# Turning gathered rows before the edge product is added, and making that product already turned, in a four-layer graph network on one core

## The chip, the core and the metric

One Trainium2 chip, one NeuronCore of it. The metric is the device time of one execution of the whole program in microseconds; lower is better. The engines are TensorE (PE, with its weight loads as PEld), VectorE (DVE), ScalarE (ACT), GpSimd (POOL) and SyncE (SP, which here only issues DMAs).

## What is computed

Four graph layers over 6250 nodes of 96 features and 206,250 edges sorted by destination, each layer followed by a layer norm of `x + layer(x)`. The change touches the edge stages of the second and third layer:

```python
# layer 1 (sum of messages)
msg  = relu(x[src] + edge_attr @ We + be)          # edge_attr: 206250 x 32, We: 32 x 96
aggr = segment_sum(msg, dst)
h    = x + aggr ...
# layer 2 (maximum of messages), twice: W1_*, then W2_*
msg  = x[src] @ W_msg + edge_attr @ W_edge
agg  = segment_max(msg, dst)                        # -inf -> 0
out  = leaky_relu(agg + x @ W_root + b)
```

Layers 0 and 3 are attention layers with edge stages of their own, which the change leaves alone.

## The kernel before

The kernel is written out fully (no loops on the chip), with waits on semaphores placed by hand; each engine runs its own list in program order.

There are five long edge stages. The first (line 789 gathers its rows) and the last (line 1843) belong to the attention layers. The three between them are made by one function, `edge_pass`: pass `e` for the sum with a ReLU (its tiles are named `e_...` in the profile, as are those of the two attention stages), passes `e2a` and `e2b` for the two maxima. Between the stages lie short node stages.

`edge_pass` walks over the edges in `NS` = 202 steps of 1024 edges. In a step:

- GpSimd issues 8 indirect DMAs (line 1151), each of which gathers 128 rows of 96 floats of `x_tab` by a column of `src_cols` into `got`. There are `RS` = 3 buffers of `got`; step s waits until the add of step s-3 has read its buffer.
- TensorE multiplies edge attributes by the edge weights (line 1168): two matmuls, the attributes as weights of the array and a block-diagonal `edge_w` (four copies of the 32 x 96 weights) streamed, 384 columns each, into the PSUM tile `EA`, edges on the partitions.
- VectorE does four things in order: `add` (line 1187: `EA` in PSUM plus `got` in SBUF, into `emsg`), `forward` (line 1193: 32 x 32 blocks turned, `emsg` into the PSUM tile `F`, so that edges lie along the free dimension), `scan` (line 1202: three scans of 256 columns, the bf16 mask in SBUF, the messages read from `F` in PSUM, into `run`), and `back` (line 1210: `run` turned back into `out`).
- In pass `e` ScalarE applies the ReLU to `emsg` between `add` and `forward` (line 1227).
- SyncE loads the attributes (one DMA a step) and the mask (four DMAs every second step) and stores `out`.

Every fourth step TensorE also makes the product of one tile of 128 nodes (line 1164, or a transposition of `X` in pass `e`) into a free corner of `EA`, and VectorE takes it out just ahead of the `add` (lines 1181 to 1185). 49 node tiles are done so in a pass.

## Time and profile before

| | |
|---|---|
| time, median of 3 runs | 11235.1 us (11234.0 to 11235.58) |
| span of the profiled execution | 13179.5 us |
| time of the profiled execution outside its span | not recorded apart |
| POOL busy | 8151.7 us (62%), 8551 instructions |
| DVE busy | 6535.8 us (50%), 10237 instructions |
| PE, PEld busy | 4527.1 us (34%), 3022.1 us (23%) |
| ACT busy | 1994.5 us (15%) |
| granted TensorE clock, mean | 0.541 of full speed |

The profiled execution is 1944 us longer than the median of the timed runs. Durations of single instructions are those of this one execution; where engines wait in it, the timed runs need not wait as long. The profile names, for each group of instructions, the busy time, the mean duration of one, and the idle time of the engine just before it with what ended that idle time: "issue" is time in which the engine waited for nothing that the profile shows, "remote" is a semaphore whose giver it did not find.

### The profile page before, as it was taken

To read this page: it belongs to the slowest core of one execution; us is meant where nothing else is said; L and a number is where in the kernel's file an instruction comes from. 1 tells how busy PE (TensorE), PEld (TensorE's weight loads), DVE (VectorE), ACT (ScalarE), POOL (GpSimd) and SP (SyncE) were. 2 spreads that over 40 slices of the span, in tenths; PEclk is the share of its full clock that TensorE was granted. 3 is DMA by queue.
4 is the path that set the end of the run, shared out by engine and by line. 5 is a ranking of instruction groups with operands and counts; after the bars stand their busy time and mean duration, and the time that the engine had idled before them with its cause. 6 is when DMAs were issued, how large, how long until landed. Compare 5 with 4: busy or idle time off the path is not lost. (4 is left out here: it accounts for less than half of the span.)

```text
span 13179.5 us, 81573 instructions
## 1 busy us (share of the span) xinstructions
PE 4527.1 (34%) x15877; PEld 3022.1 (23%) x15877; DVE 6535.8 (50%) x10237; ACT 1994.5 (15%) x4360; POOL 8151.7 (62%) x8551
## 2 busy tenths in 40 slices
PE   3354455555222222232222222222222234434443
PEld 3244344444110111111111111111111123333332
DVE  9543344444544454454445455444544544444445
ACT  3233333333100000010000000000000022222223
POOL 1455555555676666656666666766666666666665
PEclk7555555555555555555555555555555555555555
DMA  2355555555333333323333332333333222222222
GB/s 76 106 155 154 149 152 155 153 159 152 99 86 82 87 89 87 88 72 85 87 87 93 81 91 79 87 85 88 89 87 86 81 58 66 69 68 68 68 69 63
DMA packets 1007936, 1264.02 MB, mean 96 GB/s; under 512 B 483123, under 2 KB 740467, under 8 KB 1007331
## 3 DMA queue, kind: packets, MB, share of 16 engines
q0 software_dynamic: 303696, 520.91, 17.5%
q1 hardware_dynamic: 638139, 635.93, 14.8%
q10 hardware_dynamic: 65600, 101.96, 2.7%
q8 instruction: 136, 2.23, 0.1%
q14 instruction: 365, 2.99, 0.1%
HBM read 829.46 MB, written 428.44 MB: 95 GB/s over the span
## 5 line engine op out<-in xcount | busy, mean ns | idle before, releaser
L789 POOL DMA_INDIRECT e_got<-kv_tab,dst_cols x1661 | 1574.5, 948 | 1281.7 <-DVE e_pay L894 770.2
L1843 POOL DMA_INDIRECT e_got<-h_tab,src_tcols x1612 | 1540.9, 956 | 881.8 <-issue 473.8
L1151 POOL DMA_INDIRECT e2a_got<-x_tab,src_cols x1616 | 1531.3, 948 | 775.7 <-issue 556.2
L1151 POOL DMA_INDIRECT e_got<-x_tab,src_cols x1616 | 1553.5, 961 | 718.3 <-issue 586.9
L1151 POOL DMA_INDIRECT e2b_got<-x_tab,src_cols x1616 | 1531.3, 948 | 745.7 <-issue 518.8
L1168 PE MATMUL e2b_EA<-we_W_edge,e2b_attr 128*128 128x384 f32 x808 | 574.9, 866 | 1331.2 <-DVE e2b_emsg L1187 728.3
L1168 PE MATMUL e_EA<-we_We,e_attr 128*128 128x384 f32 x808 | 578.3, 871 | 1297.8 <-issue 898.1
L1168 PE MATMUL e2a_EA<-we_W_edge,e2a_attr 128*128 128x384 f32 x808 | 572.0, 862 | 1300.4 <-issue 767.3
L894 DVE TENSOR_TENSOR e_pay<-e_got,e_Q 128x384 f32<-128x384 f32 x416 | 230.2, 553 | 1570.4 <-ACT e_Q L962 1129.1
L1940 DVE TENSOR_TENSOR_SCAN e_run<-e_Z,e_run,e_msg 98x512 f32<-98x512 f32 x404 | 516.9, 1279 | 795.4 <-ACT e_msg L2005 619.8
L805 PE MATMUL e_Q<-e_window,e_pick 128*128 128x96 f32 x3328 | 758.9, 408 | 79.1 <-issue 41.2
L805 PEld LDWEIGHTS e_Q<-e_window,e_pick 128*128 128x128 f32 x3328 | 744.0, 327 | 84.8 <-issue 82.8
L812 PE MATMUL e_B<-ident,e_run 100*128 100x100 f32 x1664 | 374.5, 379 | 904.4 <-issue 493.3
L1854 PE MATMUL e_B<-ident,e_run 98*128 98x98 f32 x1616 | 357.1, 374 | 759.2 <-DVE e_run L1940 627.7
L1168 PEld LDWEIGHTS e2b_EA<-we_W_edge,e2b_attr 128*128 128x128 f32 x808 | 236.8, 323 | 1621.6 <-issue 1620.1
L829 PE MATMUL e_M<-ident,e_pay 128*100 128x128 f32 x1664 | 445.8, 422 | 470.0 <-DVE e_pay L894 366.4
L1168 PEld LDWEIGHTS e_EA<-we_We,e_attr 128*128 128x128 f32 x808 | 239.7, 327 | 1590.5 <-issue 1590.2
L1168 PEld LDWEIGHTS e2a_EA<-we_W_edge,e2a_attr 128*128 128x128 f32 x808 | 235.8, 321 | 1589.1 <-issue 1587.1
L845 DVE TENSOR_TENSOR_SCAN e_run<-e_keep,e_run,e_M 100x512 f32<-100x512 bf16 x416 | 532.3, 1280 | 11.5 <-issue 7.2
L1187 DVE TENSOR_TENSOR e2a_emsg<-e2a_EA,e2a_got 128x768 f32<-128x768 f32 x202 | 191.9, 950 | 692.4 <-remote 458.4
L1187 DVE TENSOR_TENSOR e2b_emsg<-e2b_EA,e2b_got 128x768 f32<-128x768 f32 x202 | 192.1, 951 | 671.5 <-remote 396.5
L1187 DVE TENSOR_TENSOR e_emsg<-e_EA,e_got 128x768 f32<-128x768 f32 x202 | 192.7, 954 | 648.3 <-remote 529.4
(373 smaller groups left out, 10316.0 us busy)
## 6 DMA issues: line engine op xcount, KB each, us to landing
scan_out<-e_out SPq DMA_DIRECT2D x416, 200.0 KB
e_window<-q_tab SPq DMA_DIRECT2D x1664, 48.0 KB
scan_out<-e_out SPq DMA_DIRECT2D x404, 196.0 KB
scan_out<-e_out SPq DMA_DIRECT2D x202, 384.0 KB
scan_out<-e2a_out SPq DMA_DIRECT2D x202, 384.0 KB
scan_out<-e2b_out SPq DMA_DIRECT2D x202, 384.0 KB
e_rel<-rel_row ACTq DMA_DIRECT2D x208, 256.0 KB
e_keep<-keep_row ACTq DMA_DIRECT2D x208, 200.0 KB
```

The costliest lines, as they stand in the source:

```text
L789: e.indirect_dma_start(got[i][:, k, :], None, kv_tab, bass.IndirectOffsetOnAxis(dst_c[:, c * K + k:c * K + k + 1], axis=0)).then_inc(s_g[i ...
L805: ins = e.matmul(Q[c % 3][:, k * D:(k + 1) * D], pick[c % 4][:, k, :], window[c % U][:, k, :], start=True, stop=True)
L812: ins = e.transpose(B[c % 2][:, k * PAY:(k + 1) * PAY], run[c % 3][:, k::K], ident[0:PAY, 0:PAY])
L829: ins = e.transpose(M[c % 3][0:PAY, k * P:(k + 1) * P], pay[c % 4][:, k, :], ident[:, :])
L845: e.tensor_tensor_scan(run[c % 3][:, :], keep[c // 2 % KR][:, at:at + CH], M[c % 3][0:PAY, :], run[(c + 2) % 3][:, CH - 1:CH], ALU.mult, A ...
L894: e.tensor_tensor(pay[c % 4][:, :, 0:D].rearrange("p k (h d) -> p k h d", h=HEADS), got[c % RG0][:, :, D:2 * D].rearrange("p k (h d) -> p ...
L1151: e.indirect_dma_start(got[s % RS][:, k, :], None, x_tab, bass.IndirectOffsetOnAxis(src_cols[:, q:q + 1], axis=0)).then_inc(edge_got[s % R ...
L1168: ins = e.matmul(EA[s % 2][:, h, 0:K * D], attr[s % RA][:, h * P:(h + 1) * P], edge_w[:, :], start=True, stop=True)
L1187: e.tensor_tensor(emsg[s % 3][:, :, :].rearrange("p (h k) d -> p h (k d)", h=2), EA[s % 2][:, :, 0:K * D], got[s % RS][:, :, :].rearrange( ...
L1843: e.indirect_dma_start(got[c % RG][:, k, :], None, h_tab, bass.IndirectOffsetOnAxis(src_tcols[:, q:q + 1], axis=0)).then_inc(s_g[c % RG], 16)
L1854: ins = e.transpose(B[v % 2][:, k * HW:(k + 1) * HW], run[v % 2][:, k::K], ident[0:HW, 0:HW])
L1940: V[v].give(e.tensor_tensor_scan(run[p][:, :], Z[p][0:HW, :], msg[p][:, :], run[q][:, CH - 1:CH], ALU.mult, ALU.add), "scan")
```

## The change

It regroups the three `edge_pass` stages. TensorE now uses the weights as the array's weights and streams the attributes: three matmuls of 512 columns (line 1166) make the product of two steps with the edges along the free dimension, that is already turned, into an `EA` tile of three PSUM banks. VectorE turns the gathered rows first (`forward`, line 1183, `got` in SBUF into a new SBUF tile `turned`), then adds the turned product (line 1190), and the scans (line 1199) read the sum `emsg` from SBUF. The buffer `got` is released by `forward`, no longer by `add`. The ReLU of pass `e` stands between `add` and `scan`. Node products are made four tiles at a time, every seventh block of two steps, into PSUM tiles `RT` of their own, and taken out by VectorE behind a step's `back` (`take_roots`). The attributes come in 101 DMAs of 2 KB a partition, not 202 of 1 KB. The host lays the attributes out for this, and twelve small weight loads at the program's start put the edge weights down in another block pattern.

```diff
-                F = [ph.ps(f"F{i}", [P, 2 * CH]) for i in range(2)]
+                turned = [ph.sb(f"turned{i}", [P, 3, W2]) for i in range(2)]
+                emsg = [ph.sb(f"emsg{i}", [P, 3, W2]) for i in range(3)]
+                EA = [ph.ps(f"EA{i}", [P, 3, WB]) for i in range(2)]
+                RT = [ph.ps(f"RT{i}", [P, CH]) for i in range(2)]
...
                     def _(e):
                         for s in range(NS):
-                            after(e, v_add, s - RS + 1)
+                            after(e, v_fwd, s - RS + 1)
                             for k in range(2 * K):
...
-                            for h in range(2):
-                                ins = e.matmul(EA[s % 2][:, h, 0:K * D], attr[s % RA][:, h * P:(h + 1) * P], edge_w[:, :], start=True, stop=True)
+                        for b in range(NB):
+                            e.wait_ge(s_attr[b % RA], 16 * (b // RA + 1))
+                            after(e, v_add, 2 * (b - 1))
+                            for j in range(3):
+                                ins = e.matmul(EA[b % 2][:, j, :], edge_w[:, j * P:(j + 1) * P], attr[b % RA][:, :], start=True, stop=True)
                             ins.then_inc(t_attr, 1)
+                            r = b // EVERY
+                            if b % EVERY == 0 and r < NR:
+                                after(e, root_done, r - 1)
+                                for g, q in enumerate(root_tiles(r)):
...
+                        def forward(s):
+                            e.wait_ge(edge_got[s % RS], got_before[s % RS] + 32 * K * (s // RS + 1))
+                            after(e, v_add, s - 1)
+                            e.transpose(turned_to[s % 2], blocks(got[s % RS])).then_inc(v_fwd, 1)
+
                         def add(s):
-                            e.wait_ge(t_attr, s + 1)
-                            e.wait_ge(edge_got[s % RS], got_before[s % RS] + 32 * K * (s // RS + 1))
-                            after(e, v_fwd, s - 2)
...
-                            e.tensor_tensor(emsg[s % 3][:, :, :].rearrange("p (h k) d -> p h (k d)", h=2), EA[s % 2][:, :, 0:K * D],
-                                            got[s % RS][:, :, :].rearrange("p (h k) d -> p h (k d)", h=2), ALU.add).then_inc(v_add, 1)
-
-                        def forward(s):
+                            e.wait_ge(t_attr, s // 2 + 1)
+                            e.wait_ge(v_fwd, s + 1)
+                            after(e, v_scan, s - 2)
+                            at = s % 2 * W2
+                            e.tensor_tensor(emsg[s % 3][:, :, :], EA[s // 2 % 2][:, :, at:at + W2], turned[s % 2][:, :, :], ALU.add).then_inc(v_add, 1)
...
                             for j in range(3):
-                                ins = e.tensor_tensor_scan(run[s % 3][:, j, :], mask[s // 2 % RM][:, at:at + W2], F[s % 2][:, j * W2:(j + 1) * W2],
+                                ins = e.tensor_tensor_scan(run[s % 3][:, j, :], mask[s // 2 % RM][:, at:at + W2], emsg[s % 3][:, j, :],
                                                            run[(s + 2) % 3][:, j, W2 - 1:W2], op0, op1)
...
                         for s in range(NS):
+                            forward(s)
                             add(s)
-                            forward(s)
                             scan(s)
                             back(s)
+                            if s % (2 * EVERY) == 4 and s // (2 * EVERY) < NR:
+                                take_roots(s // (2 * EVERY))
```

On VectorE, the third and fourth step of pass `e2a` before (the scans are listed as SCALAR_TENSOR_TENSOR; `F` and `EA` lie in PSUM, all else in SBUF):

```order
L1187 TENSOR_TENSOR e2a_emsg2<-e2a_EA0,e2a_got2 128x768 [waits edge_got2,edge_t_attr]
L1193 STREAM_TRANSPOSE e2a_F0<-e2a_emsg2 128x8x96 [waits edge_v_scan,edge_v_add]
L1202 SCALAR_TENSOR_TENSOR e2a_run2<-e2a_mask1,e2a_run1,e2a_F0 128x256 [waits edge_v_scan,edge_mask1,edge_v_fwd]
L1202 SCALAR_TENSOR_TENSOR e2a_run2<-e2a_mask1,e2a_run1,e2a_F0 128x256 x2
L1210 STREAM_TRANSPOSE e2a_out2<-e2a_run2 128x768 [waits edge_v_scan]
L1187 TENSOR_TENSOR e2a_emsg0<-e2a_EA1,e2a_got0 128x768 [waits edge_v_fwd,edge_got0,edge_t_attr]
```

The same place now:

```order
L1183 STREAM_TRANSPOSE e2a_turned0<-e2a_got2 128x8x96 [waits edge_v_add,edge_got2]
L1190 TENSOR_TENSOR e2a_emsg2<-e2a_EA1,e2a_turned0 128x768 [waits edge_v_fwd,edge_t_attr]
L1199 SCALAR_TENSOR_TENSOR e2a_run2<-e2a_mask1,e2a_run1,e2a_emsg2 128x256 [waits edge_v_scan,edge_mask1,edge_v_add]
L1199 SCALAR_TENSOR_TENSOR e2a_run2<-e2a_mask1,e2a_run1,e2a_emsg2 128x256 x2
L1207 STREAM_TRANSPOSE e2a_out2<-e2a_run2 128x768 [waits edge_v_scan]
L1183 STREAM_TRANSPOSE e2a_turned1<-e2a_got0 128x8x96 [waits edge_v_add,edge_got0]
```

The transposition has moved ahead of the add and writes SBUF, and the scans take all their operands from SBUF (mask, carry and messages), where they read the messages from PSUM before.

On TensorE, the first steps of pass `e2a` before (two matmuls a step, one node tile every fourth step):

```order
L1164 MATMUL e2a_EA0<-Wrc,xT_all 128x96 [waits edge_attr0]
L1168 MATMUL e2a_EA0<-we_W1_edge,e2a_attr0 128x384 x2
L1168 MATMUL e2a_EA1<-we_W1_edge,e2a_attr1 128x384 [waits edge_attr1]
L1168 MATMUL e2a_EA1<-we_W1_edge,e2a_attr1 128x384
L1168 MATMUL e2a_EA0<-we_W1_edge,e2a_attr2 128x384 [waits edge_v_add,edge_attr2]
```

and now (three matmuls for two steps, four node tiles behind the first block):

```order
L1166 MATMUL e2a_EA0<-e2a_attr0,we_W1_edge 128x512 [waits edge_attr0]
L1166 MATMUL e2a_EA0<-e2a_attr0,we_W1_edge 128x512 x2
L1173 MATMUL e2a_RT0<-Wrc,xT_all 128x96 x4
L1166 MATMUL e2a_EA1<-e2a_attr1,we_W1_edge 128x512 [waits edge_attr1]
L1166 MATMUL e2a_EA1<-e2a_attr1,we_W1_edge 128x512 x2
```

A step pair costs three weight loads where it cost four, and streams the same 1536 columns; the node tiles come in fours and no longer stand between a step's wait and its product.

## Rows read from the trace of the kernel before

**Rows 1.** The page's head: span, and busy time of each engine.

```profile
span 13179.5 us, 81573 instructions
PE 4527.1 (34%) x15877; PEld 3022.1 (23%) x15877; DVE 6535.8 (50%) x10237; ACT 1994.5 (15%) x4360; POOL 8151.7 (62%) x8551
```

**Rows 2.** Groups on POOL: busy us, mean ns | idle us before, releasers.

```profile
L789 POOL DMA_INDIRECT e_got<-kv_tab,dst_cols x1661 | 1574.5, 948 | 1281.7 <-DVE e_pay L894 770.2 <-issue 479.3 <-POOLq L354 32.2
L1151 POOL DMA_INDIRECT e_got<-x_tab,src_cols x1616 | 1553.5, 961 | 718.3 <-issue 586.9 <-DVE e_emsg L1187 117.6 <-POOLq L999 13.8
L1843 POOL DMA_INDIRECT e_got<-h_tab,src_tcols x1612 | 1540.9, 956 | 881.8 <-issue 473.8 <-ACT e_hold L2017 398.7 <-POOLq L1596 9.0
L1151 POOL DMA_INDIRECT e2a_got<-x_tab,src_cols x1616 | 1531.3, 948 | 775.7 <-issue 556.2 <-DVE e2a_emsg L1187 166.8 <-ACTq L1112 52.6
L1151 POOL DMA_INDIRECT e2b_got<-x_tab,src_cols x1616 | 1531.3, 948 | 745.7 <-issue 518.8 <-DVE e2b_emsg L1187 207.1 <-ACTq L1112 19.8
```

**Rows 3.** Timeline of one step of `e2a`: start us, duration us, instruction, idle before.

```profile
5961.91 0.95 POOL L1151 DMA_INDIRECT e2a_got<-x_tab,src_cols  x1 [0.31 <-issue]
...
5964.46 0.96 DVE L1187 TENSOR_TENSOR e2a_emsg<-e2a_EA,e2a_got 128x768 f32<-128x768 f32 x1 [4.36 <-DMA e2a_got<-x_tab,src_cols]
5965.45 0.99 DVE L1193 STREAM_TRANSPOSE e2a_F<-e2a_emsg 128x768 f32<-128x768 f32 x1
...
5966.48 2.02 DVE L1202 TENSOR_TENSOR_SCAN e2a_run<-e2a_mask,e2a_run,e2a_F 128x256 f32<-128x256 bf16 x3
5966.92 0.94 POOL L1151 DMA_INDIRECT e2a_got<-x_tab,src_cols  x1 [0.30 <-issue]
...
5968.53 1.55 DVE L1210 STREAM_TRANSPOSE e2a_out<-e2a_run 128x768 f32<-128x768 f32 x1
```

**Rows 4.** Timeline of VectorE 240 us later in `e2a`: the adds.

```profile
6193.30 0.96 DVE L1187 TENSOR_TENSOR e2a_emsg<-e2a_EA,e2a_got 128x768 f32<-128x768 f32 x1 [5.57 <-remote]
...
6204.53 0.96 DVE L1187 TENSOR_TENSOR e2a_emsg<-e2a_EA,e2a_got 128x768 f32<-128x768 f32 x1 [5.61 <-remote]
...
6232.53 0.96 DVE L1187 TENSOR_TENSOR e2a_emsg<-e2a_EA,e2a_got 128x768 f32<-128x768 f32 x1 [6.75 <-issue]
```

**Rows 5.** Groups on TensorE, VectorE (`e2a`) and ScalarE (pass `e`).

```profile
L1168 PE MATMUL e2a_EA<-we_W_edge,e2a_attr 128*128 128x384 f32 x808 | 572.0, 862 | 1300.4 <-issue 767.3 <-DVE e2a_emsg L1187 533.2
...
L1185 DVE SCALAR_TENSOR_TENSOR R<-e2a_EA,rstd_all,r_l2b 128x96 f32<-128x96 f32 x49 | 15.5, 317 | 429.2 <-remote 343.4 <-issue 52.9 <-DMA e2a_got<-x_tab,src_cols 32.8
...
L1227 ACT ACTIVATE e_emsg<-e_emsg 128x768 f32<-128x768 f32 x202 | 170.3, 843 | 2108.4 <-issue 1571.1 <-DVE e_emsg L1187 537.3
```

**Rows 6.** Timeline, start of the last edge stage: scans over a bf16 and a float tile of SBUF.

```profile
10639.40 3.52 DVE L1919 TENSOR_TENSOR_SCAN e_still<-e_keep_b,e_zeros 128x1616 f32<-128x1616 bf16 x1
10639.79 3.88 POOL L1843 DMA_INDIRECT e_got<-h_tab,src_tcols  x1 [0.30 <-issue]
...
10642.84 3.50 DVE L1921 TENSOR_TENSOR_SCAN e_ad_e<-e_keep_b,e_first 128x1616 f32<-128x1616 bf16 x1
...
10643.98 3.11 POOL L1843 DMA_INDIRECT e_got<-h_tab,src_tcols  x1 [0.30 <-issue]
```

**Rows 7.** Timeline in the last edge stage: a short scan of that form, one of 101.

```profile
10727.68 0.47 DVE L1970 TENSOR_TENSOR_SCAN e_rm<-e_neg_t,e_rm,e_zl 16x128 f32<-16x128 bf16 x1
10727.81 1.09 POOL L1843 DMA_INDIRECT e_got<-h_tab,src_tcols  x1 [0.30 <-issue]
```

**Rows 8.** Timeline at the program's start: operations with both inputs in SBUF.

```profile
25.06 1.02 DVE L607 TENSOR_TENSOR prep_A<-prep_A 128x832 f32<-128x832 f32 x1
25.21 1.69 POOL L428 DMA_INDIRECT R<-in_dst_pad,prep_row_i  x1 [0.30 <-issue]
```

**Rows 9.** Source line 1961, the 128-column scan from SBUF: ns min/median/max, first and last start.

```profile
L1961 DVE TENSOR_TENSOR_SCAN e_own<-e_neg_t,e_zl x101: 411/411/414, 10664.2 to 13066.2; 16x128 f32<-16x128 bf16 x101
```

**Rows 10.** Timeline, end of pass `e2a`: its last gather, and VectorE's last step.

```profile
8096.66 0.94 POOL L1151 DMA_INDIRECT e2a_got<-x_tab,src_cols  x1 [0.30 <-issue]
...
8107.12 0.96 DVE L1187 TENSOR_TENSOR e2a_emsg<-e2a_EA,e2a_got 128x768 f32<-128x768 f32 x1 [4.17 <-remote]
...
8111.20 1.55 DVE L1210 STREAM_TRANSPOSE e2a_out<-e2a_run 128x768 f32<-128x768 f32 x1
```

More of the change, by code:

```diff
@@ L1129, in _ @@
                         load_mask(0)
-                        for s in range(1, RA):
-                            load_attr(s)
+                        for b in range(1, RA):
+                            load_attr(b)
                         load_mask(1)
                         for s in range(NS):
-                            if s + RA < NS:
-                                load_attr(s + RA)
-                            if s % 2 == 0 and s // 2 + 2 < NB:
-                                load_mask(s // 2 + 2)
+                            if s % 2 == 0:
+                                b = s // 2
+                                if b + RA < NB:
+                                    load_attr(b + RA)
+                                if b + 2 < NB:
+                                    load_mask(b + 2)
                             if s >= 2:
@@ L1191, in forward, with scan @@
+                            e.tensor_tensor(emsg[s % 3][:, :, :], EA[s // 2 % 2][:, :, at:at + W2], turned[s % 2][:, :, :], ALU.add).then_inc(v_add, 1)
+                        def scan(s):
                             e.wait_ge(a_relu if relu else v_add, s + 1)
-                            after(e, v_scan, s - 1)
-                            e.transpose(turned[s % 2], blocks(emsg[s % 3])).then_inc(v_fwd, 1)
-                        def scan(s):
-                            e.wait_ge(v_fwd, s + 1)
@@ L1210, in back, with take_roots @@
                             e.transpose(blocks(out[s % 3]), run_back[s % 3]).then_inc(v_back, 1)
+                        def take_roots(r):
+                            e.wait_ge(t_root, r + 1)
+                            tiles = root_tiles(r)
+                            n, q0 = len(tiles), tiles[0]
+                            raw = RT[r % 2][:, 0:n * P].rearrange("p (g c) -> p g c", c=P)[:, :, 0:D]
+                            if root is None:
+                                ins = e.tensor_copy(xT_all[:, q0 * P:(q0 + n) * P], RT[r % 2][0:D, 0:n * P])
+                            elif root_scale is None:
+                                ins = e.tensor_tensor(R[:, q0:q0 + n, :], raw, root_bias[:, :].unsqueeze(1).to_broadcast([P, n, D]), ALU.add)
+                            else:
+                                for g, q in enumerate(tiles):
+                                    ins = e.scalar_tensor_tensor(R[:, q, :], raw[:, g, :], root_scale[:, q:q + 1], root_bias[:, :], ALU.mult, ALU.add)
+                            ins.then_inc(root_done, 1)
                         e.memset(run[2][:, :, :], 0.0).then_inc(s_init, 1)
```

59 lines of the change are left out of this document (22 added, 37 removed).

## Prediction

> **What bounds the kernel now.** I read the page's head first. No engine is near full: POOL is busiest with 62%, DVE has 50% [rows 1]. So I looked for the engine whose waits end last, stage by stage. The groups on POOL say most: the five long streams of gathers together hold 8121 recorded gathers (8128 by the program: 1664 + 4 x 1616) and, busy and idle before them added, 2856 + 2272 + 2423 + 2307 + 2277 = 12,135 us of the 13,179.5 us [rows 2]. All else is the remaining 1045 us.
>
> How fast can POOL go? Where nothing holds it, a gather has 0.945 us and 0.30 us of "issue" before it, so one each 1.25 us [rows 3]. 8128 x 1.25 = 10,160 us, and with the other 1045 us that is 11,205 us: 30 us under the median of the timed runs, 11,235.1. The profiled execution is 1944 us above it, and the waits that its streams hold over the bare pace are 12,135 - 10,160 = 1975 us, about the same amount. My reading: the timed runs go at POOL's pace from the first gather of each stream to its last, and have next to none of the waits that the profile shows.
>
> What those waits are: in part of pass `e2a` the adds come 11.23 us apart, or 28.00 us for two steps with a node tile between them [rows 4], ended by "remote", where eight gathers need only 10.0. The groups show TensorE's matmuls at 0.862 us each, four records a step, 3.4 us [rows 5]; yet the add waits for their semaphore. So the profiled execution is held by TensorE in such stretches. That can't be so for long in the timed runs unless a gather costs them under 1.25 us, since 11,205 leaves no room. Sums below are made on the bare pace, and set against 11,235, not against 13,179.5.
>
> **The change, part by part.**
>
> *TensorE.* Per two steps 4 matmuls of 384 columns become 3 of 512: the same columns, one weight load less. Worth something only where TensorE holds the add, that is, by the reading above, nothing: its cover is POOL's 20 us for two steps. In the profiled execution it is worth up to a quarter of 11.2 us a step.
>
> *Node products.* 49 operations of 0.317 us a pass [rows 5] ahead of an add become 13 groups behind a `back`. VectorE's step is 0.96 + 0.99 + 2.02 + 1.55 us [rows 3], 5.6 us of 10.0 with its gaps, so this is hidden, before and after. Four node products in a row (1.3 us) still fit.
>
> *Attribute DMAs.* 101 for 202 with the same bytes, three blocks (six steps) ahead: SP has fewer waits in front of its stores; hidden. The twelve weight loads in smaller pieces are in the preparation, ahead of any use by two stages: nothing. `got` comes free after `forward`, at about the time the add freed it, and POOL needs it two steps later: nothing. At a pass's end there is one VectorE chain behind the last gather, as before [rows 10]: at most +0.6 us a pass, for the transposition below.
>
> *The transposition.* It now reads `got` and writes SBUF in pieces 8 floats apart. Before, with the same write pattern into PSUM, it took 0.99 us; `back`, which reads SBUF with that stride and writes it straight, takes 1.55 us [rows 3]. So 0.99 to 1.55 us. By itself hidden: VectorE's step would be 6.1 us at most, 7.0 with the ReLU's 0.843 us [rows 5], of 10.0.
>
> The Trainium skill ("Advanced Engine Details and Errata", Memory Cachelines) says that accesses to SBUF that meet another 16-byte line each time pay a penalty; by it the transposition would be at the 1.55 end. That agrees with `back` here, which reads so; it does not tell about writes.
>
> *The scans.* This is the part that costs. Their own length hardly changes: from SBUF a scan of 128 columns takes 0.411 us [rows 9] and one of 1616 takes 3.52 [rows 6], which gives 0.68 for 256, and three took 2.02 from PSUM [rows 3]. But they now have both inputs, mask and messages, in SBUF, and the trace shows what such an instruction does to a gather. A gather that starts 0.39 us into a 3.52 us scan of this form lasts 3.88 us, and ends 0.75 us after the scan; the next, behind 3.50 us of another scan, lasts 3.11 us, again ending 0.75 us after it [rows 6]. Behind a short one, 1.09 us instead of 0.945 [rows 7]. Behind an add of two SBUF tiles, 1.69 us, 0.82 after the add's end [rows 8]. Today's scans, with the messages in PSUM, don't: the gather inside them lasts 0.94 [rows 3]. So the gather asks for something 0.13 to 0.20 us after its start, I take 0.15, and gets it only when the running instruction of this kind ends. None of the present instructions of `edge_pass` is of this kind, since `add` reads `EA` from PSUM.
>
> The Trainium skill ("SBUF — State Buffer", Who interferes with whom) has both sides: a DVE instruction with two SBUF inputs contends with a GpSimd one that reads SBUF; but it infers that `tensor_tensor` leaves descriptor generation alone, since that needs the write interface. By the first the wait is real, by the second it is nought. The trace agrees with the first for these gathers [rows 6 to 8].
>
> Now the places. Take the start of a step's last gather as 0. The add came at 2.55 (5964.46 - 5961.91) [rows 3]; now `forward` starts there. With 0.99 us for it, the add starts at 3.57 and the scans fill 4.56 to 6.58, each a third. The next step's gathers start at 1.25, 2.50, 3.75, 5.00, 6.25. The one at 5.00 asks at 5.15 and waits for the first scan's end, 5.23: 0.08 us. The next then asks at 6.48 and waits 0.10 for the third scan. Sum 0.18 us. With 1.55 us for `forward` the scans fill 5.12 to 7.14: the ask at 5.15 waits 0.64, the next again 0.10, sum 0.74 us. In the sum pass ReLU and its hand-over add some 0.87 us: there 0.38 (scans from 5.43) or 0.36 us (from 5.99). POOL is the bound, so all of it adds up. Over the passes: 202 x (0.18 + 0.18 + 0.38) = 149 us with the quick transposition, 202 x (0.74 + 0.74 + 0.36) = 372 us with the slow one. If landings shift so much that the place is arbitrary: an ask falls into the first scan with 0.67/1.25 = 0.54 and costs 0.34 + 0.10, else into the second for 0.39: 0.42 us a step, 254 us. That lies between the two; I take 250 us.
>
> **Sum:** 11,235 + 250 = 11,485 us, 2.2% slower. Bounds: 149 and 372 give 11,384 and 11,607; the most a step can lose is 0.67 + 0.10 us, 11,702 in all.
>
> **The rivals.**
>
> *A: the gathers wait behind the scans* (the forecast): 11,485 us. For it: the gathers behind such instructions [rows 6 to 8], and that the bare pace closes to 30 us. Against: the placing of the waits is by arithmetic to a tenth of a microsecond.
>
> *B: faster.* The timed runs do wait for TensorE as in the profile, and gathers cost less there than in it: (11,235 - 1045 - 1975) / 8128 = 1.01 us. Then a step's product at 11.2 us would fall to between 8.4 (three matmuls for four) and 11.2 us (by columns). A pass is 2285 us on average, and 202 x 8.4 + 49 x 5.6 (28.00 - 2 x 11.2 for a node tile) = 1971 us at best: up to 314 us a pass, 940 us in all; half of it, since TensorE does not hold all steps, gives 10,765 us. It decides where TensorE's step takes longer than eight gathers. For it: the "remote" waits [rows 4]. Against: it needs a gather pace that no row shows, and the closure at 1.25 would be an accident.
>
> *C: no change.* What the gathers ask for is not what the new scans hold, or they slip through between two scans at no cost: 11,235 us. The inference of the Trainium skill's page named above is this case. For it: the waits of 0.08 to 0.10 us are small beside the scatter of landings. Against: one place or another is hit in every step.
>
> **How the numbers follow.** A 0.79, B 0.13, C 0.08. A's own range is 11,370 to 11,620. The full range must leave out no more than 2 in 10: it reaches from 11,215, just under C, to 11,650, some way to A's limit; outside are B and a little of A. 0.2% is 22 us, about what a measurement of this kernel can tell from no change; all of A is above it. Faster 0.13, same 0.08, slower 0.79.
>
> **What would show it.** In the changed kernel's profile the gathers of the three passes should have a mean of 970 to 1040 ns (0.18 to 0.74 us over eight gathers) where they have 948 to 961, with single ones of 1.0 to 1.6 us that end 0.75 us behind a scan's end; the group of line 1183 tells which transposition it is, 0.99 or 1.55. Since the waits on TensorE there shrink, the profiled span may well get shorter, by up to some 450 us, while the timed runs get longer: that would be the clearest sign that the profile's waits on TensorE are not in the timed runs. Wrong I am if the gathers keep their 945 ns beside the scans, or if the timed runs fall with the profiled span (B).

## The result and the profile after

The changed kernel takes 11,338.8 us (median of 4 runs, 11,336.7 to 11,342.6), the kernel before 11,235.3 us beside it (11,234.0 to 11,236.4). The ratio is 1.0093, 95% interval 1.008 to 1.0105: 103 us slower. Forecast were 11,485 us, 250 us slower.

The page of the changed kernel, head and groups (line engine op, tiles, count | busy us, mean ns | idle us before, releaser):

```profile
span 11340.7 us, 79536 instructions
PE 4072.4 (36%) x15271; PEld 2736.6 (24%) x15271; DVE 6875.8 (61%) x10165; ACT 2008.8 (18%) x4360; POOL 8198.2 (72%) x8551
...
L790 POOL DMA_INDIRECT e_got<-kv_tab,dst_cols x1661 | 1573.2, 947 | 538.2 <-issue 478.2
L1156 POOL DMA_INDIRECT e2a_got<-x_tab,src_cols x1616 | 1550.0, 959 | 546.9 <-issue 492.2
L1156 POOL DMA_INDIRECT e_got<-x_tab,src_cols x1616 | 1575.7, 975 | 506.2 <-issue 492.3
L1156 POOL DMA_INDIRECT e2b_got<-x_tab,src_cols x1616 | 1550.7, 960 | 507.0 <-issue 492.1
L1856 POOL DMA_INDIRECT e_got<-h_tab,src_tcols x1612 | 1528.9, 948 | 500.2 <-issue 491.0
...
L1166 PE MATMUL e2a_EA<-e2a_attr,we_W_edge 128*128 128x512 f32 x606 | 500.6, 994 | 1506.4 <-DVE e2a_emsg L1190 1496.5
...
L1183 DVE STREAM_TRANSPOSE e2a_turned<-e2a_got 128x768 f32<-128x768 f32 x202 | 314.2, 1555 | 767.5 <-DMA e2a_got<-x_tab,src_cols 767.5
```

This execution runs as the timed ones do: its span is 11,340.7 us. GpSimd's idle time before gathers is nearly all "issue", 0.30 us for each, where before it also waited for `add` and others [rows 2]. `forward` waits for the gathered rows alone and TensorE waits for `add`. So GpSimd sets the time, and what the change costs must stand in the gathers' own durations: 959, 960 and 975 ns in the three passes that it touches. A gather that nothing holds has 944 in this trace. 1616 x 0.944 = 1525.5 us, so gathers were held for 24.5, 25.2 and 50.2 us in the passes `e2a`, `e2b` and `e`, 99.9 us together, and the time is 103 us longer.

The profile of before that the prediction read is slower than this one by 1839 us although its kernel is the faster. The section on the other chips below deals with that. An execution of the kernel before on one of the quicker chips is the first experiment.

### The profile page after: what moved, and what is told of

Read it like the earlier page. It is cut to its first block and busy times, and to the rows that moved or that the text cites. A ratio compares the mean times of both kernels' runs of the same rounds, so it can differ in the third digit from the quotient of the medians.

```text
span 11340.7 us, 79536 instructions
## 1 busy us (share of the span) xinstructions
PE 4072.4 (36%) x15271; PEld 2736.6 (24%) x15271; DVE 6875.8 (61%) x10165; ACT 2008.8 (18%) x4360; POOL 8198.2 (72%) x8551
## 5 line engine op out<-in xcount | busy, mean ns | idle before, releaser
L1166 PE MATMUL e_EA<-e_attr,we_We 128*128 128x512 f32 x606 | 515.5, 1020 | 1600.3 <-DVE e_emsg L1190 1513.8
L1166 PE MATMUL e2a_EA<-e2a_attr,we_W_edge 128*128 128x512 f32 x606 | 500.6, 994 | 1506.4 <-DVE e2a_emsg L1190 1496.5
L1166 PE MATMUL e2b_EA<-e2b_attr,we_W_edge 128*128 128x512 f32 x606 | 499.5, 992 | 1505.8 <-DVE e2b_emsg L1190 1499.0
L1183 DVE STREAM_TRANSPOSE e2b_turned<-e2b_got 128x768 f32<-128x768 f32 x202 | 314.1, 1555 | 774.0 <-DMA e2b_got<-x_tab,src_cols 774.0
L1183 DVE STREAM_TRANSPOSE e2a_turned<-e2a_got 128x768 f32<-128x768 f32 x202 | 314.2, 1555 | 767.5 <-DMA e2a_got<-x_tab,src_cols 767.5
L1183 DVE STREAM_TRANSPOSE e_turned<-e_got 128x768 f32<-128x768 f32 x202 | 314.1, 1555 | 622.6 <-DMA e_got<-x_tab,src_cols 622.6
L878 DVE TENSOR_TENSOR e_prod<-e_Q,e_got 128x384 f32<-128x384 f32 x416 | 231.1, 555 | 695.6 <-DMA e_got<-kv_tab,dst_cols 677.1
L1166 PEld LDWEIGHTS e_EA<-e_attr,we_We 128*128 128x128 f32 x606 | 183.6, 323 | 1918.4 <-issue 1831.6
L1166 PEld LDWEIGHTS e2b_EA<-e2b_attr,we_W_edge 128*128 128x128 f32 x606 | 182.2, 321 | 1807.9 <-issue 1801.0
L1199 DVE TENSOR_TENSOR_SCAN e_run<-e_mask,e_run,e_emsg 128x256 f32<-128x256 bf16 x606 | 411.6, 735 | 183.9 <-ACT e_emsg L1240 183.9
```

What stands on the lines that cost most here:

```text
L878: e.tensor_tensor(prod[:, :, :], Q[c % 3][:, 0:K * D].rearrange("p (k d) -> p k d", k=K), got[c % RG0][:, :, 0:D], ALU.mult).then_inc(v_pr ...
L1166: ins = e.matmul(EA[b % 2][:, j, :], edge_w[:, j * P:(j + 1) * P], attr[b % RA][:, :], start=True, stop=True)
L1183: e.transpose(turned_to[s % 2], blocks(got[s % RS])).then_inc(v_fwd, 1)
L1199: ins = e.tensor_tensor_scan(run[s % 3][:, j, :], mask[s // 2 % RM][:, at:at + W2], emsg[s % 3][:, j, :], run[(s + 2) % 3][:, j, W2 - 1:W2 ...
```

## The hold of a gather, row by row

Timeline of two steps of `e2a` in the changed kernel (start us, duration us, instruction; x3 are three scans, 0.64 to 0.67 us from one to the next, 0.73 to 0.75 us each):

```profile
5000.67 1.56 DVE L1183 STREAM_TRANSPOSE e2a_turned<-e2a_got 128x768 f32<-128x768 f32 x1 [1.31 <-DMA e2a_got<-x_tab,src_cols]
...
5002.32 0.96 DVE L1190 TENSOR_TENSOR e2a_emsg<-e2a_EA,e2a_turned 128x768 f32<-128x768 f32 x1
...
5003.31 2.04 DVE L1199 TENSOR_TENSOR_SCAN e2a_run<-e2a_mask,e2a_run,e2a_emsg 128x256 f32<-128x256 bf16 x3
5004.42 1.03 POOL L1156 DMA_INDIRECT e2a_got<-x_tab,src_cols  x1 [0.30 <-issue]
...
5015.73 2.04 DVE L1199 TENSOR_TENSOR_SCAN e2a_run<-e2a_mask,e2a_run,e2a_emsg 128x256 f32<-128x256 bf16 x3
5015.74 0.94 POOL L1156 DMA_INDIRECT e2a_got<-x_tab,src_cols  x1 [0.30 <-issue]
5016.99 0.94 POOL L1156 DMA_INDIRECT e2a_got<-x_tab,src_cols  x1 [0.30 <-issue]
```

The gather at 5004.42 is held: the second scan runs from 5003.98 to 5004.70, and the gather ends at 5005.45, 0.75 us after it, as in [rows 6]. The gather at 5015.74 is not, though the first scan began 0.02 us before it and runs for another 0.73 us. By the prediction's rule (it asks 0.15 us after its start, and waits for whatever then runs) it would have been held 0.58 us. All such pairs in this trace, worked out from the records: of 325 gathers whose step's first scan began between 0.05 us before their start and 0.30 us after it, none lasts over 0.954 us; of the 96 whose first scan began 0.10 to 0.25 us before them, none lasts under 1.251. So the law that the trace shows is this: **a gather is held by an instruction that began at least 0.1 us before it and ends more than 0.2 us after its start; it then ends 0.75 us after that instruction.** The edge is not sharp. In the traces from the quicker chips no gather was held by a scan that began less than 0.04 us before it, every one was by a scan that began 0.10 us or more before it (with enough of it left), and in between it varies: here 10 of the 24 that a scan preceded by 0.06 to 0.10 us.

For the second and third scans of a step that run when a gather starts, by what is left of them (rounded to 0.1 us; the last row has scans that had hardly begun, and mixes held gathers with free ones):

```
rest of the scan (us)   gathers   mean duration (us)
0.1                       63      0.943
0.2                      276      0.974
0.3                      173      1.054
0.4                       49      1.137
0.5                       19      1.248
0.6                       19      1.358
0.7                       15      1.070
```

A scan of 0.73 us that began 0.10 us ahead has 0.63 left and holds a gather for 0.63 + 0.75 - 0.944 = 0.44 us; the longest gather among these lasts 1.419 us, 0.475 over a free one. The prediction had 0.67 for the most that one scan can hold.

The law was read in this trace. Applied to each of its 4848 gathers at the place where it really stands, with the edge at 0.085 us, it gives 102 us of holds (measured 99.9), and all but 12 gathers last within 0.03 us of what it says.

## Experiments on chips with the kernel before at 11,235 us

**The kernel before again.** No edit.

> The kernel before once more, for a profile. Theory 1 (the five gather streams go at POOL's pace of 1.25 us a gather in timed runs, and the waits on TensorE in the first profile belonged to that execution alone): the time is 11,235 us, and if this profile is free of those waits each stream of 1616 gathers has 1.250 us from gather to gather, about 2020 us in all, and a mean gather of 945 ns. Rival (timed runs wait for TensorE, and gathers are quicker in them): whenever the span is near 11,235 us the gathers come less than 1.25 us apart and VectorE's adds still end waits on TensorE.

It took 11,256.7 us in its one run, span 11,254.9 (the median of the kernel before on this chip is 11,235.3). From its page:

```profile
L1151 POOL DMA_INDIRECT e2a_got<-x_tab,src_cols x1616 | 1528.4, 946 | 546.8 <-issue 492.5
...
L1168 PE MATMUL e2a_EA<-we_W_edge,e2a_attr 128*128 128x384 f32 x808 | 581.2, 875 | 999.0 <-DVE e2a_emsg L1187 999.0
...
L1187 DVE TENSOR_TENSOR e2a_emsg<-e2a_EA,e2a_got 128x768 f32<-128x768 f32 x202 | 193.0, 955 | 594.3 <-DMA e2a_got<-x_tab,src_cols 594.3
```

`add` waits for gathered rows, TensorE for `add`, nobody for TensorE: rival B's premise is not met where the kernel is timed, and GpSimd goes at 1.25 us a gather from end to end. Its gathers take 946 ns where other executions have 944; over 8128 gathers that is 16 us, most of the 21 us by which this run is above the others.

**The sum goes back into PSUM.** Everything of the change stays (turned products, `forward` first into SBUF, node products in fours), but `add` writes `EA` in place and the scans read it there. Two things follow that the cut of the edit leaves out: the ReLU of pass `e` works in `EA` too, and TensorE waits for the scans, not the add, of the block whose `EA` it overwrites.

```diff
-e.tensor_tensor(emsg[s % 3][:, :, :], EA[s // 2 % 2][:, :, at:at + W2], turned[s % 2][:, :, :], ALU.add)
+e.tensor_tensor(EA[s // 2 % 2][:, :, at:at + W2], EA[s // 2 % 2][:, :, at:at + W2], turned[s % 2][:, :, :], ALU.add)
...
-e.tensor_tensor_scan(run[...], mask[...], emsg[s % 3][:, j, :], ...)
+e.tensor_tensor_scan(run[...], mask[...], EA[s // 2 % 2][:, j, at:at + W2], ...)
```

> The changed kernel, but the add writes its sum back into the PSUM tile EA, and ReLU and scans read it there; TensorE waits for the scans of two blocks before. All other parts of the change stay: transposition first and into SBUF at 1.55 us, three matmuls for two steps, node products in fours, attribute DMAs of 2 KB. Theory 1 (gathers are held by scans with both inputs in SBUF): the loss of 93 us in the gather streams goes, 11,235 to 11,250 us, mean gather 945 ns. Theory 2 (the loss comes from the other parts: longer VectorE chain, later landings, DMA bursts): about 11,335 us as the changed kernel.

**The scans in six pieces of 128 columns**, from SBUF as in the changed kernel:

```diff
-for j in range(3):
-    ins = e.tensor_tensor_scan(run[s % 3][:, j, :], mask[...], emsg[s % 3][:, j, :], run[(s + 2) % 3][:, j, W2 - 1:W2], op0, op1)
+for h in range(2):
+    lo = h * CHS
+    for j in range(3):
+        start = run[s % 3][:, j, CHS - 1:CHS] if h else run[(s + 2) % 3][:, j, W2 - 1:W2]
+        ins = e.tensor_tensor_scan(run[s % 3][:, j, lo:lo + CHS], mask[...], emsg[s % 3][:, j, lo:lo + CHS], start, op0, op1)
+    if h == 0:
+        ins.then_inc(v_half, 1)
+        e.wait_ge(v_half, s + 1)
```

> The changed kernel with each scan of 256 columns cut into two of 128, six a step (0.41 us each), still both inputs in SBUF. Theory 1 in its exact form (a gather is held only by a scan that began at least 0.1 us before it and ends over 0.2 us after its start, and until that scan's end): a scan of 0.41 us can hold a gather for 0.12 us at most, and the placing gives some 11 us over the three passes in place of 101: 11,245 to 11,260 us. Theory 3 (scans and gathers share a port by bandwidth, so the loss goes with the time for which they overlap): the scans' time together grows from 2.0 to 2.4 us a step, so the loss stays or grows, 11,335 to 11,355 us. Theory 2: as the changed kernel, some 11,340 us.

**The kernel before with its scans' input in SBUF.** One line of the kernel before, so nothing of the change but this:

```diff
-F = [ph.ps(f"F{i}", [P, 2 * CH]) for i in range(2)]
+F = [ph.sb(f"F{i}", [P, 2 * CH]) for i in range(2)]
```

> The kernel before with one edit: the tile F, into which VectorE turns the sums and from which the scans read, lies in SBUF in place of PSUM. No other part of the change is there. Theory 1: the scans now have both inputs in SBUF, the transposition takes 1.55 us, and the chain add, transposition, scans stands at the same place as in the changed kernel: 11,235 + 80 to 110 us, that is 11,315 to 11,345, mean gather 955 to 975 ns. Theory 2 (loss from the new product layout, bursts, node products): 11,235 to 11,245 us.

| beside 11,235.3 us | us | ratio, 95% interval |
|---|---|---|
| sum back in PSUM | 11,238.1 | 1.0003 (0.9993 to 1.0012) |
| six scans of 128 | 11,272.0 | 1.0033 (1.002 to 1.0045) |
| before, `F` in SBUF | 11,356.3 | 1.0107 (1.009 to 1.0124) |

The gathers of pass `e` on the three pages, in this order:

```profile
L1155 POOL DMA_INDIRECT e_got<-x_tab,src_cols x1616 | 1524.8, 944 | 506.2 <-issue 492.3
```

```profile
L1157 POOL DMA_INDIRECT e_got<-x_tab,src_cols x1616 | 1541.8, 954 | 506.3 <-issue 492.4
...
L1203 DVE TENSOR_TENSOR_SCAN e_run<-e_mask,e_run,e_emsg 128x128 f32<-128x128 bf16 x1212 | 499.4, 468 | 191.1 <-ACT e_emsg L1247 183.8
```

```profile
L1151 POOL DMA_INDIRECT e_got<-x_tab,src_cols x1616 | 1582.4, 979 | 506.2 <-issue 492.3
```

With the scans' messages in PSUM the loss is gone and every gather is back at 944 ns, while all else of the change is kept; with one tile of the kernel before in SBUF the loss is there (in pass `e` 1582.4 - 1525.5 = 57 us, 50 in the changed kernel) without anything else of the change. That settles the cause. The size was missed: 121 us in all, where 80 to 110 were expected.

Twice as many scans of half the length lose 37 us where three lose 103: it is not the number of overlaps that costs, but what is left of a scan. Expected were 10 to 25. They took 468 ns each and not the 411 of [rows 9], so the most that one can hold a gather is, by the law, 0.37 + 0.75 - 0.944 = 0.17 us and not 0.12; whether that is the whole of the miss is not shown. (Its profile can't be set against 944 ns: the commonest gather in it takes 947, as in the kernel before again. Against that profile the three passes' gathers take 29 us more.) The 0.06 us are not a matter of the partitions: the scan of [rows 7] has 16 partitions too and takes 0.47. It begins, as those of `edge_pass` do, from a value in a tile, and the one of [rows 9] from a constant; no run changes that alone.

**How the hold depends on a scan's length and place.** Three kernels, on another chip where the kernel before took 11,241.7 us. One scan of 768 columns for three of 256 (it leaves out the mask, reading a constant row in its place, and lets the running value go on from one segment into the next):

```diff
-for j in range(3):
-    e.tensor_tensor_scan(run[s % 3][:, j, :], mask[...], emsg[s % 3][:, j, :], ...)
+e.tensor_tensor_scan(flat(run[s % 3]), wide[:, :], flat(emsg[s % 3]), ...)
```

> One scan of 768 columns for three of 256 (its output is not the reference's), once more for a chip where the kernel before takes 11,235 us. Hold law: 530 us over the kernel before, 11,700 to 11,800 us. A fixed price for each overlap: under 11,339. The chain's length as the cause: 11,339. On a chip of 13,150 us: 0.997, nothing told apart.

Later scans, by a copy behind the add (`EA` is now read behind the add, so TensorE waits for the scans and not the add; the cut leaves that out):

```diff
 e.tensor_tensor(emsg[...], EA[...], turned[...], ALU.add)
+e.tensor_copy(spare[:, :], EA[s // 2 % 2][:, 0, at:at + 128])
```

> A copy of 0.28 us between add and scans, once more. Hold law: 45 to 58 us in each maximum pass, 48 to 50 in the sum pass, 11,370 to 11,400 us. A fixed price: 11,339. The chain's length: up to 11,460. On a chip of 13,150 us: 0.997, nothing told apart.

A transposition that writes straight (the columns then stand in another order than the product's, so it adds the wrong pairs):

```diff
-turned[i][:, :, :].rearrange("p j (e k) -> p k j e", k=2 * K)
+turned[i][:, :, :].rearrange("p j w -> p (j w)").rearrange("p (k j f) -> p k j f", k=2 * K, j=3)
```

> The gathered rows transposed without interleaving, 0.98 us for 1.555 (its output is not the reference's), once more. Hold law: 110 to 127 us over the kernel before, 11,345 to 11,365 us. The chain's length as the cause: below 11,300 us. On a chip of 13,150 us: 0.997, nothing told apart.

| beside 11,241.7 us | us | ratio, 95% interval |
|---|---|---|
| one scan of 768 | 11,697.0 | 1.0405 (1.0388 to 1.0422) |
| later scans | 11,340.5 | 1.0084 (1.0067 to 1.0101) |
| straight transposition | 11,341.2 | 1.0087 (1.007 to 1.0103) |

Groups, and a timeline of `e2a`, of the kernel with one scan:

```profile
L1157 POOL DMA_INDIRECT e_got<-x_tab,src_cols x1616 | 1739.4, 1076 | 506.1 <-issue 492.3
L1157 POOL DMA_INDIRECT e2a_got<-x_tab,src_cols x1616 | 1638.9, 1014 | 547.1 <-issue 492.2
...
L1200 DVE TENSOR_TENSOR_SCAN e_run<-e_wide,e_run,e_emsg 128x768 f32<-128x768 bf16 x202 | 367.3, 1818 | 183.8 <-ACT e_emsg L1241 183.8
```

```profile
6204.41 0.94 POOL L1157 DMA_INDIRECT e2a_got<-x_tab,src_cols  x1 [0.30 <-issue]
6204.49 1.82 DVE L1200 TENSOR_TENSOR_SCAN e2a_run<-e2a_wide,e2a_run,e2a_emsg 128x768 f32<-128x768 bf16 x1
...
6205.66 1.41 POOL L1157 DMA_INDIRECT e2a_got<-x_tab,src_cols  x1 [0.30 <-issue]
...
6216.76 1.82 DVE L1200 TENSOR_TENSOR_SCAN e2a_run<-e2a_wide,e2a_run,e2a_emsg 128x768 f32<-128x768 bf16 x1
6217.37 1.97 POOL L1157 DMA_INDIRECT e2a_got<-x_tab,src_cols  x1 [0.30 <-issue]
```

The gather at 6204.41 started 0.08 us ahead of the scan and goes free. The next one ends at 6207.07, 0.76 us after the scan's end at 6206.31; the one at 6217.37 ends at 6219.34, 0.76 us after 6218.58. So the law holds for another length, and one long instruction costs 455 us where three short ones cost 103: a fixed price for each overlap has fallen. At the gathers' real places the law gives 448 us of holds for this kernel, and 445 are measured. Worked through step by step with fixed landings (the time from the start of a step's last gather until its rows are there) it had given 530: 213 for the sum pass, where 214 came, but 160 for each maximum pass, where 113 and 118 came.

Groups of the kernel with later scans, and one step of it, then groups of the one with the straight transposition:

```profile
L1157 POOL DMA_INDIRECT e_got<-x_tab,src_cols x1616 | 1577.1, 976 | 506.0 <-issue 492.2
L1157 POOL DMA_INDIRECT e2a_got<-x_tab,src_cols x1616 | 1546.0, 957 | 547.0 <-issue 492.2
```

```profile
5002.74 0.96 DVE L1191 TENSOR_TENSOR e2a_emsg<-e2a_EA,e2a_turned 128x768 f32<-128x768 f32 x1
5003.62 0.28 DVE L1192 COPY e2a_spare<-e2a_EA 128x128 f32<-128x128 f32 x1
5003.81 2.02 DVE L1201 TENSOR_TENSOR_SCAN e2a_run<-e2a_mask,e2a_run,e2a_emsg 128x256 f32<-128x256 bf16 x3
```

```profile
L1156 POOL DMA_INDIRECT e_got<-x_tab,src_cols x1616 | 1576.1, 975 | 506.1 <-issue 492.2
L1156 POOL DMA_INDIRECT e2a_got<-x_tab,src_cols x1616 | 1546.1, 957 | 547.2 <-issue 492.2
...
L1183 DVE STREAM_TRANSPOSE e2a_turned<-e2a_got 128x768 f32<-128x768 f32 x202 | 197.6, 978 | 880.7 <-DMA e2a_got<-x_tab,src_cols 880.7
```

Both missed what was expected of them. The longer chain on VectorE is not the cause: 0.58 us less in each of 606 steps gives nothing.

The copy did not do what it was put in for. The scans begin 1.07 us behind the add's start (5003.81 - 5002.74) where they began 0.99 behind it in the changed kernel (5003.31 - 5002.32): 0.08 us later, not 0.2. Against the gathers they are not later at all. Median starts of the first scan of `e2a`, from the start of the step's last gather: 7.3 and 5.2 us in turn in the changed kernel, 6.3 and 5.1 with the copy, 6.2 and 4.5 with the straight transposition. In the steps of the first number the rows themselves are there about 1 us (copy) or 0.3 to 0.5 us (straight) sooner in these two profiles, and why is not known. So these two kernels don't test one chosen shift; they show three placings of the scans that cost nearly the same, 99, 99 and 103 us.

Gather for gather the law holds in both traces (of 318 and 168 gathers with a first scan from 0.05 us before to 0.30 after their start, none lasts over 0.953 us; at the real places it gives 93 and 98 us of holds, and 93 and 94 are measured). What was wrong is the placing: it could not be had by arithmetic from a few landings. The three scans are some 0.66 us apart and gathers 1.25, so wherever they fall, one scan or another is running behind some gather's start.

## Eight runs on two other chips

The same three kernels, one more, and the changed kernel itself ran on two chips on which the kernel before takes 13,155.2 and 13,149.2 us, 17% longer. On the first of them also one in which each of the three scans is done twice, the first time into a spare tile:

```diff
 for j in range(3):
+    e.tensor_tensor_scan(spare[:, j, :], mask[...], emsg[s % 3][:, j, :], ...)
+for j in range(3):
     e.tensor_tensor_scan(run[s % 3][:, j, :], ...)
```

Two of the texts call the chip of 13,155.2 us, the first here, "the second chip", since the one of 11,235.3 us came before it.

> The changed kernel with the three scans of 256 columns in one scan of 768, both inputs in SBUF (it leaves out the mask: a constant row is read in its place, and the three running results aren't kept apart). Fewer instructions and less VectorE time (about 1.8 us in place of 2.04 a step). Theory 1 in its exact form (a gather is held until the end of the scan that runs as it starts): the scan can hold a gather for 1.5 us; with the landings of the profiles (2.5 and about 4.4 us behind the last gather, in turn) my arithmetic gives 150 to 155 us in each maximum pass and 205 in the sum pass, 11,750 us in all. Theory 3 (loss by time of overlap): a little less than the changed kernel, 11,320 to 11,340 us.

> The changed kernel with the three scans of a step made twice, the first time into a spare tile: 4.05 us of them a step. Theory 1 in its exact form: about 45 us in each maximum pass and 60 in the sum pass in place of 23 and 48, so 11,385 us. Theory 3 (loss by time of overlap): twice the loss, 11,440 us.

> The changed kernel with the forward transposition writing its result straight on, not in pieces 8 floats apart (the 32 x 32 blocks are turned, but their elements are not interleaved by edge, so the sums are of other elements). It tells what the 1.555 us of that transposition are: the write stride, then it takes about 0.99 us; SBUF as target, then it stays at 1.55. With 0.99 us the scans start 0.56 us earlier, and by the exact form of theory 1 the maximum passes lose 35 us each and the sum pass 59 (23 and 48 now): 11,365 us. If the chain's length were what costs, it would get faster: under 11,335 us.

> The changed kernel with a copy of 128 columns out of PSUM between add and scans (one input, in PSUM; TensorE waits for the scans of two blocks before). It moves the scans of the maximum passes some 0.29 us later; in the sum pass it hides behind the ReLU. Theory 1 in its exact form: loss of a maximum pass 23 -> 50 to 58 us, sum pass unchanged at 48 to 50, so about 11,390 us. Any theory that counts instructions or time of overlap: no change by the place, 11,340 us.

On the second chip:

> The changed kernel itself, unaltered, as the anchor for the three kernels that run beside it. The run of four experiments on the second chip (kernel before 13,155 us there) could not show what each does to the gathers' holds in the time, since every version ended its passes at 2,235 us there. Theory 1 with the hold law read from the changed kernel's trace (a gather is held only if a scan began at least 0.1 us before it, and then till 0.75 us after the end of that scan): 1.009 of the kernel before on a chip where the kernel before takes about 11,235 us (11,325 to 11,350 us). On a chip where the kernel before takes about 13,150 us: 0.996 to 1.001, because something other than POOL's own pace sets the end there.

> The changed kernel with one scan of 768 columns (1.82 us by the trace of this kernel on the second chip) in place of three of 256; it leaves out the mask's segments and carries the running value from segment to segment, so its output is not the reference's. By the hold law the gather that comes inside the scan waits for the end of the whole of it, so holds grow from 0.1 to 0.47 us to as much as 1.6 us a step: worked through step by step with landings 2.5 and 4.4 us after the last gather, 160 us in each maximum pass and 213 us in the sum pass, 530 us in all: 11,700 to 11,800 us on a chip where the kernel before takes 11,235 us. Theory 2 (a fixed price for each scan that overlaps a gather, whatever its length): fewer scans, fewer holds, so under 11,339 us, about 11,270 to 11,300. Theory 3 (the loss is the transposition's, 0.57 us a step longer than thought, and no hold): 11,339 as the changed kernel. On a chip where the kernel before takes 13,150 us: 0.996, as before, and nothing told apart.

> The changed kernel with a copy of 128 columns (0.28 us) between the add and the scans, so that the scans of the maximum passes start about 0.2 us later against the gathers; in the sum pass the copy lies beside ScalarE's relu and moves nothing. By the hold law the later start puts longer rests of the scans behind a gather's start in the maximum passes: 45 to 58 us each in place of 25, and 48 to 50 in the sum pass as in the changed kernel: 11,370 to 11,400 us. Theory 2 (a fixed price for each overlapping scan): no change against the changed kernel, 11,335 to 11,345. Theory 3 (a longer chain on VectorE is what costs): at most 202 x 3 x 0.2 us = 120 us more, 11,460. On a chip where the kernel before takes 13,150 us: 0.997 and nothing told apart.

> The changed kernel with the gathered rows transposed straight, without the interleaving of the columns, so that the transposition takes 0.98 us in place of 1.555; its output is not the reference's, since the columns are in the other order. The scans start 0.57 us earlier against the gathers. By the hold law: 30 to 35 us in each maximum pass and 51 to 58 in the sum pass, 110 to 127 in all against 101: 11,345 to 11,365 us, no gain although VectorE does 0.57 us less in each of 606 steps. Theory 3 (the longer transposition is what costs): a part of 606 x 0.57 = 348 us comes back, below 11,300 us, and all of the loss if the chain on VectorE is the whole cause. On a chip where the kernel before takes 13,150 us: 0.996 and nothing told apart.

| | first chip, us | ratio, 95% interval | second chip, us | ratio, 95% interval |
|---|---|---|---|---|
| changed kernel | | | 13,120.2 | 0.9973 (0.9961 to 0.9984) |
| one scan | 13,113.6 | 0.9965 (0.995 to 0.9979) | 13,117.2 | 0.9973 (0.9956 to 0.9991) |
| scans twice | 13,186.0 | 1.0014 (1.0001 to 1.0027) | | |
| straight | 13,103.3 | 0.9956 (0.9939 to 0.9973) | 13,102.5 | 0.9969 (0.9956 to 0.9981) |
| later scans | 13,118.9 | 0.997 (0.9958 to 0.9983) | 13,111.2 | 0.9969 (0.9957 to 0.998) |

The sizes expected on the first chip all missed, since they were reckoned on a chip of 11,235 us. On the second chip what was expected for a chip of 13,150 us came: 0.996 to 1.001, nothing told apart. Pass `e` on the second chip, of the changed kernel and of the one with one scan:

```profile
L1156 POOL DMA_INDIRECT e_got<-x_tab,src_cols x1616 | 1710.7, 1059 | 539.8 <-issue 526.0
```

```profile
L1157 POOL DMA_INDIRECT e_got<-x_tab,src_cols x1616 | 1742.8, 1078 | 507.8 <-issue 494.0
```

Busy and idle together are 2250.5 and 2250.6 us: the gathers take longer with the long scan and their idle time shrinks by as much. The straight and the later scans come to the same within 1 us. So here something other than GpSimd's own pace lets one gather pass each 1.39 us, and a hold is made good behind it. Only the kernel with its scans done twice is outside of this (1564.0 + 708.1 = 2272.1 us): there GpSimd waits 144.0 us for `forward` to free a buffer. In the timeline of the changed kernel there, gathers of 0.95 and of about 1.09 us stand in a row behind the held one at 5003.03, with no scan beside them:

```profile
5003.03 1.54 POOL L1156 DMA_INDIRECT e_got<-x_tab,src_cols  x1 [0.30 <-issue]
5004.87 1.11 POOL L1156 DMA_INDIRECT e_got<-x_tab,src_cols  x1 [0.30 <-issue]
5006.28 1.08 POOL L1156 DMA_INDIRECT e_got<-x_tab,src_cols  x1 [0.30 <-issue]
5007.67 1.09 POOL L1156 DMA_INDIRECT e_got<-x_tab,src_cols  x1 [0.30 <-issue]
5009.07 0.95 POOL L1156 DMA_INDIRECT e_got<-x_tab,src_cols  x1 [0.30 <-issue]
```

What it is stays open. The gathers' rows land no later there than on the quicker chips (1.16 us behind the gather's end at the median, by the records of the transfers, against 1.25), so nothing shows a queue of transfers piling up. The profile of before, of this kind too by its span (13,179.5 us), shows `add` waiting for TensorE [rows 4]: in `e2a` TensorE's signal that a step's product is done comes 10.1 us behind the start of its matmuls (median of the 156 signals recorded), where it comes after 2.9 us in the repeated profile of before. These waits are gone in the changed kernel. VectorE's waits in 2100 us of `e2a`, before and then in the changed kernel on the second chip:

```profile
DVE e2a_emsg L1187 <- remote: 423.4, 76, 6.8
DVE R L1185 <- remote: 335.1, 36, 10.5
```

```profile
DVE e2a_turned L1183 <- DMA e2a_got<-x_tab,src_cols: 760.6, 164, 6.4
DVE e2a_turned L1183 <- issue: 143.1, 25, 6.5
DVE e2a_emsg L1190 <- DVE e2a_turned L1183: 0.9, 2, 0.4
```

The pass gets little from it, from first gather to last 2236 us for 2254, since the pace of one gather each 1.39 us lies just behind. And more than half of what a slower chip costs lies in the two attention stages, which the change leaves alone: their gathers go from first to last in 2867 and 2414 us, against 2140 and 2020 in the first profile of the changed kernel. No run here was made to tell what the causes are, nor whether it is the chips that differ or the times at which they were used: no chip is on record in both ways.

## Why the prediction was right and wrong

- **The bound (1.25 us a gather, waits of the profile not in the timed runs): right.** The repeated profile of before has no such wait. The reason behind those waits was not seen: the profiled execution was, by its time, of the slower kind, which takes some 13,150 us for every version.
- **TensorE, node products, attribute DMAs, release of `got`: nothing. Right.** With the scans' input in PSUM all of it together is 1.0003 (0.9993 to 1.0012).
- **The transposition: 0.99 to 1.55 us, hidden. Right, at the upper end**, 1.555. The cost lies in the write pattern: written straight it takes 0.978. The Trainium skill ("Advanced Engine Details and Errata", Memory Cachelines) speaks of accesses that meet another 16-byte line each time, and this agrees with it for writes: 1.555 us against 0.978.
- **The scans hold gathers: right in kind.** The inference of the Trainium skill ("SBUF — State Buffer", Who interferes with whom) that `tensor_tensor` leaves descriptor generation alone, carried over to these scans, does not fit: 11,338.8 with both inputs in SBUF, 11,238.1 with one in PSUM.
- **The failed step is the size of that term**: "So the gather asks for something 0.13 to 0.20 us after its start, I take 0.15, and gets it only when the running instruction of this kind ends." [Rows 6 to 8] are all of instructions that had begun 0.13 us or more ahead of the gather; none has one that begins between the gather's start and 0.15 us later, and that case is free. The prediction had 0.74 us a step for the maximum passes with the slow transposition, 0.64 of it from just that case, and 0.36 for the sum pass. Measured are 24.5 / 202 = 0.12 and 50.2 / 202 = 0.25. The average for an arbitrary place, 0.42, from which the 250 us came, was too high for the same reason: by the law one scan holds 0.44 us at most and falls to nothing within 0.44 us of starts, so three of them hold about 3 x 0.44 x 0.44 / 2 / 1.25 = 0.23 us a step, an estimate; 606 steps of it are 140 us, not 254, for 103 measured.
- **Second, one landing was taken for all.** [Rows 3] show a step whose last gather starts 2.55 us ahead. In the changed kernel that is 2.5 us in every second step and 4.1 to 4.7 (medians of the passes) in the others. Worked through in the prediction's way with the 1.555 us and landings of 2.5 and 4.4, the old rule gives 326 us, so the landing alone does not mend the sum. The law gives 67 us so, 97 to 101 with 4.1 or 4.7 for the 4.4: with fixed landings it comes near the 103 in part by luck, and at the real places of the gathers it gives 102.
- **Signs that were named.** The mean gather was to be 970 to 1040 ns: it is in one pass (975), and below in two (959 and 960). Single gathers that end 0.75 us behind a scan came as named. The profiled span did get shorter while the timed runs got longer, but the two profiles are of the two kinds of execution, so this sign came by luck and shows nothing of TensorE's waits.
- **Rival B** needs a chip of the slower kind. There the adds' waits for TensorE do go, but the change gains 0.27%, some 30 us and nowhere near the 470, since the gathers' pace of that kind comes next. **Rival C** fell.

## What to carry to other kernels

Where GpSimd's indirect gathers are the bound, look at every VectorE instruction with two inputs, both in SBUF, that can run beside them (scans, and adds as in [rows 8]; the transpositions, with their single input in SBUF, held nothing). It costs a gather what is left of the instruction at the gather's start, less 0.19 us. So keep one input in PSUM, or keep these instructions short, and count neither the other engines' savings nor the instruction's own length. Before a rule for a wait is put into a sum, look for rows on both sides of its edge: rows that all show the wait cannot say where it stops. And when the profiled execution and the timed ones differ by 17%, ask first whether they are of the same kind.

## What was not expected of the hardware

- The chips of these runs fall into two kinds for this program: the kernel before takes 11,235 and 11,242 us on two, 13,149 and 13,155 on two others (or did at the times when they were used), and the sign of this change differs between them (1.0093 and 0.9973).
- A gather is not held by a scan that begins with it or less than 0.04 us ahead, and always by one that began 0.10 us ahead and is long enough; 0.75 us are left after a hold, for scans of 0.47 to 3.5 us.
- A transposition of 768 columns into SBUF takes 0.978 us written straight and 1.555 in pieces 8 floats apart; into PSUM the same pieces take 0.99 [rows 3].
- A scan of 128 columns takes 468 ns on 128 partitions and 473 on 16 [rows 7] when it begins from a value in a tile, 411 on 16 when it begins from a constant [rows 9]; that this is the reason is not shown.
